# Attention probabilities of layer three transposed by DMA in two 16-bit planes instead of by TensorE

## The reference

```
def _cross_attention(q_in, kv_in, wq, bq, wk, bk, wv, bv, wo, bo, bias_k, bias_v):
    b, q_len, _ = q_in.shape
    t = kv_in.shape[1]
    qh = (q_in @ wq + bq).reshape(b, q_len, H, K)
    kh = (kv_in @ wk + bk).reshape(b, t, H, K)
    vh = (kv_in @ wv + bv).reshape(b, t, H, K)
    kh = jnp.concatenate([kh, jnp.broadcast_to(bias_k, (b, 1, H, K))], axis=1)
    vh = jnp.concatenate([vh, jnp.broadcast_to(bias_v, (b, 1, H, K))], axis=1)
    logits = jnp.einsum('bqhk,bthk->bhqt', qh, kh) / scale
    weights = jax.nn.softmax(logits, axis=-1)
    ctx = jnp.einsum('bhqt,bthk->bqhk', weights, vh).reshape(b, q_len, H * K)
    return ctx @ wo + bo
```

## Time and profile before

| | |
|---|---|
| median of 3 runs | 2156.26 us (2155.0 to 2164.39) |
| profiled execution, its own time | 2160.24 us |
| its span | 2158.5 us |
| mean granted clock of TensorE | 0.965 of full speed |
| PE / PEld / DVE / ACT / POOL busy | 90% / 76% / 50% / 44% / 33% |
| items of layer three's attention | 128, scores from 500 to 1554 us |

### The profile page before, as it was taken

How to read it: one execution, slowest core, us unless ns; L and a number is a source line. 1 busy time by engine, 2 the same in 40 slices (tenths; PEclk the granted TensorE clock), 3 DMA queues, 4 the chain that set the end, 5 groups by cost and what they waited for, 6 DMA issues and landing times.

```text
span 2158.5 us, 39293 instructions
## 1 busy us (share of the span) xinstructions
PE 1932.7 (90%) x16097; PEld 1644.8 (76%) x16097; DVE 1080.9 (50%) x1979; ACT 956.9 (44%) x2550; POOL 707.7 (33%) x819
## 2 busy tenths in 40 slices
PE   6788887898999999999999999999989788878798
PEld 4566665786888888888888888888867666657587
DVE  4444544544444444455554444445443577686743
ACT  4244333333444444343434443444434467666633
POOL 3322222402232413234233241323321367666500
PEclk9899998999999999999999999999999899999899
DMA  3000001100000000000001010000020000000000
GB/s 107 10 7 2 7 2 41 57 1 20 10 30 1 30 11 11 21 1 21 11 19 42 1 40 1 17 14 1 20 87 1 10 2 1 7 1 6 1 19 22
DMA packets 28035, 38.45 MB, mean 18 GB/s; under 512 B 1344, under 2 KB 19408, under 8 KB 27856
## 3 DMA queue, kind: packets, MB, share of 16 engines
q1 hardware_dynamic: 27856, 35.95, 5.2%
HBM read 33.84 MB, written 2.10 MB: 17 GB/s over the span
## 4 chain that ended last, share of the span: by engine, by line
PE 77%; DVE 10%; ACT 8%; issue 3%; POOL 1%; DMA 0%; ACTq 0%; SPq 0%; DVEq 0%; POOLq 0%
PE ps_high L196 40%; PE ps_four L196 7%; PE ps_four L2613 5%; PE ps_four L2633 5%; PE ps_four L2622 2%; PE ps_four L2417 2%; PE ps_high L2509 2%; PE ps_high L2400 1%; ACT l_pt L1717 1%; PE ps_four L2425 1%; PE ps_four L2539 1%; PE ps_high L2438 1%; ACT l_pt L1759 1%; DVE l_sm L2134 1%; PE ps_four L2549 1%
## 5 line engine op out<-in xcount | busy, mean ns | idle before, releaser
L1813 ACT ACTIVATE l_prob<-ps_four,l_mx 128x129 f32<-128x129 f32 x512 | 181.7, 368 | 565.3 <-DVE l_mx L2169 565.3
L1605 POOL TENSOR_TENSOR l_prob<-l_prob,l_mx 128x516 f32<-128x516 f32 x128 | 134.4, 1050 | 723.2 <-DVE l_mx L2176 723.2
L196 PE MATMUL ps_high<-ctxT,l_wk 128*128 128x512 f32 x768 | 211.9, 412 | 0.0
L196 PE MATMUL ps_high<-l_hT,l_wq 128*128 128x512 f32 x768 | 209.8, 408 | 0.0
L196 PEld LDWEIGHTS ps_high<-l_wo,l_ao 128*128 128x128 f32 x1536 | 196.3, 189 | 14.0 <-DVE l_ao L2188 3.1
L196 PE MATMUL ps_high<-l_wo,l_ao 128*128 128x256 f32 x1536 | 202.3, 281 | 1.9 <-DVE l_ao L2188 1.9
L196 PE MATMUL ps_high<-l_wv,ctxT 128*128 128x512 f32 x768 | 201.8, 398 | 1.8 <-ACT l_qT L1794 1.4
L1571 POOL TENSOR_TENSOR l_sm<-l_sm,l_mask 128x1024 f32<-128x1024 f32 x64 | 150.3, 2370 | 119.8 <-DVE l_sm L2134 119.6
L196 PEld LDWEIGHTS ps_high<-l_wv,ctxT 128*128 128x128 f32 x768 | 143.0, 189 | 44.0 <-ACT l_qT L1794 10.3
L196 PEld LDWEIGHTS ps_high<-ctxT,l_wk 128*128 128x128 f32 x768 | 137.2, 192 | 23.1
L196 PEld LDWEIGHTS ps_high<-l_hT,l_wq 128*128 128x128 f32 x768 | 134.6, 188 | 22.9
(11 more groups left out here) (296 smaller groups left out, 3878.6 us busy)
## 6 DMA issues: line engine op xcount, KB each, us to landing
l_staging<-in_L_xattn_wv SPq DMA_DIRECT2D x8, 512.0 KB, 3.6
l_staging<-in_L_xattn_wk SPq DMA_DIRECT2D x8, 512.0 KB, 3.6
l_staging<-in_L_xattn_wq SPq DMA_DIRECT2D x8, 512.0 KB, 4.0
l_staging<-in_L_xattn_wo SPq DMA_DIRECT2D x8, 512.0 KB, 3.5
ctx_tok<-in_ctx SPq DMA_DIRECT2D x8, 256.0 KB, 3.3
x_tok<-in_x SPq DMA_DIRECT2D x4, 512.0 KB, 5.5
l_raw_w<-in_L_xattn_mlp_w SPq DMA_DIRECT2D x2, 1024.0 KB, 7.5
l_staging<-in_L_xattn_w_fc SPq DMA_DIRECT2D x4, 512.0 KB, 4.1
```

The source lines that it names most:

```text
L196: ins = e.matmul(out, a, b, start=start and i == 0, stop=stop and i == 2, skip_group_check=not check)
L1605: e.tensor_tensor(pr[:, :, 0:S + 1], pr[:, :, 0:S + 1], mx[:, 3, :].unsqueeze(2).to_broadcast([P, GB, S + 1]), ALU.mult).then_inc(sem("poo ...
L1813: ins = e.activation(pr.t[:, b, 0:S + 1], banks[b // 2].t[:, (b % 2) * (S + 2):(b % 2) * (S + 2) + S + 1], ACT.Exp, bias=mx[:, 1, b:b + 1] ...
```

## The change

The four transposes on TensorE and the copy out of PSUM go. VectorE now splits the scaled probabilities of item step-1, seen as 16-bit halves, into two planes (low and high halves), SyncE turns both by one transposing DMA of 128 x 1024 elements of 16 bits, and VectorE merges the two turned planes into `l2_probT` in the next step. To make room, the buffers for queries and keys become one each instead of two; there is one buffer for the planes and one for the turned planes.

The order in a step is new. After the scores (step-1) come the low part of the output of item step-3 (`rest`), the merge (step-2), the query and the key projection (step), the normalisation and the split into planes (step-1), the output projection of item step-3, one batch of V, and the values (step-2) last. Since GpSimd writes the key columns with the stage of the key projection, these now stand ahead of its scaling. The weight loads are issued by ScalarE instead of SyncE, and the next weights are asked for two items earlier. The layer normalisations' transposes use bank 2 alone. In the second attention one bias matmul of 256 columns stands in place of two of 128. `x_bias` now waits for the bias loads of each layer.

```diff
-        QT = self.ring("l2_qT", 2, [P, T], F32, scope)
-        KT = self.ring("l2_kT", 2, [P, GB, S + 2], F32, scope)
+        QT = self.ring("l2_qT", 1, [P, T], F32, scope)
+        KT = self.ring("l2_kT", 1, [P, GB, S + 2], F32, scope)
+        planes = [Slot(sb("l2_planes" + n, [P, 2, GB, S], U16)) for n in ("", "T")]
...
-            if g == 1 and h == 0 and nxt[0] < 2 and nxt not in wslots:
+            if g == 0 and h == 2 and nxt[0] < 2 and nxt not in wslots:
...
+        self.tr = self.banks(2)
...
         for step in range(N + 2):
             if 1 <= step <= N:
                 scores(step - 1)
+            if 3 <= step:
+                rest(step - 3)
+            if 2 <= step:
+                merge(step - 2)
             if step < N:
                 project(step, "q")
+            if step < N:
+                project(step, "k")
+            else:
+                next(mlp)
+                next(mlp)
             if 1 <= step <= N:
                 normalise_rows(step - 1)
-            if 2 <= step <= N + 1:
-                values(step - 2)
+                transposes(step - 1)
+            if 3 <= step:
+                output(step - 3)
+            advance(weights_ahead, 1)
+            advance(norms_ahead, 4 if step < 12 else 2)
+            project(step - 2, "v")
             if step >= N:
                 next(mlp)
                 next(mlp)
-            advance(weights_ahead, 1)
-            advance(norms_ahead, 4 if step < 12 else 2)
-            if step < N:
-                project(step, "k")
-            project(step - 2, "v")
-            if 2 <= step <= N + 1:
-                output(step - 2)
-            if step >= N:
-                next(mlp)
-                next(mlp)
-            if 1 <= step <= N:
-                transposes(step - 1)
+            if 2 <= step:
+                values(step - 2)
+        rest(N - 1)
+        output(N - 1)
         self.barrier("l3")
...
+        def l2_tr(n):
+            f = pl.info["l2_tr", n]
+            q.wait_ge(*pl.done("dve.l2_planes", n))
+            q.wait_ge(*(pl.done("dve.l2_merge", n - 1) if n else pl.event(f["free"])))
+            e.dma_start(self.planes[1][:].rearrange("p i b t -> p (i b) t"), self.planes[0][:].rearrange("p i b t -> p (i b t)"),
+                        transpose=True).then_inc(sem("sp.l2_tr"), 16)
...
+        def l2_planes(n):
+
+            q.wait_ge(*pl.done("pool.l2_norm:n", n))
+            q.wait_ge(*(pl.event(pl.info["l2_tr", n - 1]["landed"]) if n else pl.event(pl.info["l2_planes", n]["free"])))
+            e.tensor_copy(self.planes[0][:], use["l2_prob", n].t[:, :, 0:S].bitcast(U16).rearrange(
+                "p b (t i) -> p i b t", i=2)).then_inc(sem("dve.l2_planes"), 1)
+
+        def l2_merge(n):
+            pt = use["l2_probT", n]
+            q.wait_ge(*pl.event(pl.info["l2_tr", n]["landed"]))
             q.wait_ge(*pl.event(pt.before))
-            e.tensor_copy(pt.t[:], bk.t).then_inc(bk.slot.empty, 1)
+            e.tensor_copy(pt.t[:].bitcast(U16).rearrange("p (b t i) -> p b t i", b=GB, i=2),
+                          self.planes[1][:].rearrange("p i b t -> p b t i")).then_inc(sem("dve.l2_merge"), 1)
...
-        def l2_tr(n):
-            pr = use["l2_prob", n].t
-            q.wait_ge(*pl.done("pool.l2_norm:n", n))
-            bk = fill("l2_tr", n)
-            for b in range(GB):
-                ins = e.transpose(bk.t[:, b * S:(b + 1) * S], pr[:, b, 0:S], self.ident[:])
-            ins.then_inc(bk.slot.full, 1)
```

More of the change, by code:

```diff
@@ L784, in plan_l2_attention @@
         hT = [Ring([Slot(sb("l2_hT3", [P, 2, DC, T], F32R))])]
-        QT = self.ring("l2_qT", 2, [P, T], F32, scope)
-        KT = self.ring("l2_kT", 2, [P, GB, S + 2], F32, scope)
+        QT = self.ring("l2_qT", 1, [P, T], F32, scope)
+        KT = self.ring("l2_kT", 1, [P, GB, S + 2], F32, scope)
+        planes = [Slot(sb("l2_planes" + n, [P, 2, GB, S], U16)) for n in ("", "T")]
+        self.planes = [s.t for s in planes]
         PR = self.ring("l2_prob", 2, [P, GB, S + 2], F32, scope)
         late = [s for k in (PT, AO, pbT, hT[0], QT, KT, PR) for s in k.slots]
+        late += planes
         hT2 = Ring([Slot(sb("l2_hT2", [P, 2, DC, T], F32R))])
@@ L839, in load_mlp_weights @@
                 i = staging.slots.index(pl.use["l2_staging", "l2m", name, part].slot)
-                pl.emit("m_w_load", name, part, landed=self.dma(f"sp.l2_staging{i}"))
+                pl.emit("m_w_load", name, part, landed=self.dma(f"act.l2_staging{i}"))
                 for half in range(2):
@@ L921, in transposes, with merge @@
         def transposes(n):
-            pl.bank(tr_ring, "l2_tr", n)
+            pl.emit("l2_planes", n, free=planes[0].freed if n == 0 else None)
+            pl.free("l2_prob", n, by=("dve.l2_planes", n))
+            pl.emit("l2_tr", n, landed=self.dma("sp.l2_tr"), free=planes[1].freed if n == 0 else None)
+        def merge(n):
             pl.slot(PT, "l2_probT", n)
-            pl.emit("l2_tr", n)
-            pl.free("l2_tr", n)
-            pl.free("l2_prob", n, by=("full", "l2_tr", n))
+            pl.emit("l2_merge", n)
         def values(n):
@@ L938, in values, with rest @@
                 pl.free("V", n - h, by=("full", "l2_values", n))
+        def rest(n):
+            pl.emit("l2_rest", n)
+            pl.free("l2_values", n)
         def output(n):
@@ L1371, in l2_loads @@
             e.dma_start(self.l2m_b2[:], a["L2_xattn_b_fc2"].partition_broadcast(P)).then_inc(sem("sp.l2m_bias"), 16)
[L1373 to L1387, removed]
-                src = a["L2_xattn_w_fc1"].rearrange("(c p) n -> p c n", p=P)[:, :, part * F // 2:(part + 1) * F // 2]
-            else:
-                src = a["L2_xattn_w_fc2"].rearrange("(c p) n -> p c n", p=P)[:, part * FC // 2:(part + 1) * FC // 2, :]
-            e.dma_start(u.t[:].rearrange("p (c n) -> p c n", c=src.shape[1]), src).then_inc(
-                sem(pl.info["m_w_load", name, part]["landed"][1]), 16)
+        def l2_tr(n):
[4 more added lines that the diff above has]
+                        transpose=True).then_inc(sem("sp.l2_tr"), 16)
         def l3_loads():
@@ L1824, in l2_values, with l2_w_load, m_w_load @@
                 sem("act.l2_values"), 1)
+        def l2_w_load(k, at, hg):
+            u, n = use["l2_staging", k, at, hg], str(at + 1)
+            q.wait_ge(*pl.event(u.before))
+            if k == "wo":
+                src = self.a["L2_xattn_wo" + n][hg * HG * K2:(hg + 1) * HG * K2, :].rearrange("(c p) n -> p c n", p=P)
+                dst = u.t[:].rearrange("p (c n) -> p c n", c=HG)
+            else:
+                src = self.a[f"L2_xattn_{k}{n}"].rearrange("(c p) n -> p c n", p=P)[:, :, hg * HG * K2:(hg + 1) * HG * K2]
+                dst = u.t[:].rearrange("p (c n) -> p c n", c=DC)
+            e.dma_start(dst, src).then_inc(sem(pl.info["l2_w_load", k, at, hg]["landed"][1]), 16)
+        def m_w_load(name, part):
+            u = use["l2_staging", "l2m", name, part]
+            q.wait_ge(*pl.event(u.before))
+            if name == "w1":
+                src = self.a["L2_xattn_w_fc1"].rearrange("(c p) n -> p c n", p=P)[:, :, part * F // 2:(part + 1) * F // 2]
+            else:
+                src = self.a["L2_xattn_w_fc2"].rearrange("(c p) n -> p c n", p=P)[:, part * FC // 2:(part + 1) * FC // 2, :]
+            e.dma_start(u.t[:].rearrange("p (c n) -> p c n", c=src.shape[1]), src).then_inc(
+                sem(pl.info["m_w_load", name, part]["landed"][1]), 16)
         def l2_pbT(at, g):
@@ L2627, in l2_values @@
             v, pt = use["V", n - h].t, use["l2_probT", n].t
-            q.wait_ge(*pl.event(("empty", "l2_tr", n)))
+            q.wait_ge(*pl.done("dve.l2_merge", n))
             for b in range(GB):
@@ L2671, in l2_out_bias @@
             n = self.items.index((at, H2 // HG - 1, g, 0))
-            pt, parts = use["pbT", at, g].t, 2 if at else 1
+            pt = use["pbT", at, g].t
             q.wait_ge(*pl.event(("empty", "l2_pbT", at, g)))
@@ L2676, in l2_out_bias @@
                 bk = use["side", ("l2", n), b // 2]
-                for c in range(parts):
-                    lo = c * D // parts
-                    ins = e.matmul(bk.t[:, (b % 2) * D + lo:(b % 2) * D + lo + D // parts], pt[:, b, :],
-                                   self.BWs[:, lo:lo + D // parts], start=False, stop=True, skip_group_check=True)
+                ins = e.matmul(bk.t[:, (b % 2) * D:(b % 2 + 1) * D], pt[:, b, :], self.BWs[:], start=False, stop=True,
+                               skip_group_check=True)
             ins.then_inc(sem("pe.l2_out_bias"), 1)
```

27 lines of the change are left out of this document (12 added, 15 removed).

## The result

The changed kernel takes 2088.21 us in the median of four runs (2083.72 to 2094.77), the kernel before 2159.62 us on the same chips (2155.0 to 2164.39): the ratio is 0.9672, 95% interval 0.9635 to 0.9708. The profiled execution has a span of 2082.0 us.

A forecast was written before the change was run, and what follows sets the result against it. TensorE's own work was taken to bound the attention steps. The terms -55 - 8 + 0 + 3 + 3 + 3 gave -54 us, so 2106 us against the profiled execution and 2102 us against the median; range 2085 to 2255 us.

The forecast's parts named there:

- Transposes, -55 us: Layer three's attention: four transposes per item leave TensorE, 0.43 us in each of 128 steps, all on the path.
- VectorE copies: Split into planes and merge on VectorE: 0.69 us each, at most 1.38 us; no bound by VectorE's sum.
- The transfer: Transposing DMA between split and merge: taken as 3.3 us from issue, like a 256 KB load; bounds 2.0 and 7.5 us.
- The loop: Merge, reciprocal, scaling, split and transfer come round once a step: 2.9 us + L, 6.3 us, under TensorE's 7.37 us.
- The first rival: The loop becomes the bound from L = 4.9 us, making the kernel slower, about 2260 to 2450 us; chance 0.26.
- L: Time from the split's end to the turned data being there, SP's issue included; taken as 3.4 us.
- Small stalls, -8 us: Steps after an x addition: V's 0.40 us wait for the query evacuation shrinks, some 30 x 0.25 us back.
- normalisations, 0: Normalisation steps: the wait for the values' bank goes, waits for ScalarE's copy come; set against each other, within 10 us.
- Key columns first: GpSimd writes the key columns ahead of its scaling: costs nothing, moves 0.2 us ahead of a wait.
- GpSimd +3: VectorE's split meets GpSimd's weight splits and both slow: loop 7.0 to 7.6 us in half the steps, +3 us.
- loads +3: Weight loads on ScalarE's queue: issue hidden, but sharing DMA engines they can hold up a transfer, +3 us.
- Tail, +3 us: After the last scores, little covers the two copies, the transfer and the output's added step: about 3 us longer.

The follow-up runs named there:

- a_pe_transposes: Changed kernel with planes, transfer and merge taken out and TensorE's four transposes put back behind the values: stage 1028.4 us, ratio to before 0.9869.
- p_out_of_order: Changed kernel with a plain transfer, the split writing both planes in turn in the order of its reads: stage 1074.5 us, ratio to before 1.0102.
- a_no_transfer: Changed kernel without the transposing transfer, the merge reading the unturned planes, both VectorE copies kept: stage 983.8 us, ratio to before 0.9669.
- p_weights_on_sp: Changed kernel with a plain transfer, weight loads issued by SyncE again instead of ScalarE: stage 981.9 us, ratio to before 0.9624.

## Why the prediction was right or wrong

The sign and the mechanism (TensorE bounds the stage, the transfer stays hidden) were right, the size a quarter too small. In part the nearness is luck, as errors of opposite sign cancel: the transposes gave 10 us less than the sum has, the order 17 us more than its 8, and the terms for GpSimd, loads and tail were 9 us of loss where the stage shows 2 at most and the tail a gain of 3. By its steps:

- **Transposes, -55 us.** Right in a plain step: 7.81 became 7.40 us in the traced one, and in the new order the eleven plain sums are shorter by 0.44 us a step without the transposes. Over the stage, moving the transposes is worth 44.6 us in the new order, as the normalisation steps keep only 6 of their 17 us: PE stands still 5.9 us longer than in a_pe_transposes and the granted clock falls again. That VectorE's extra copies delay these steps is likely, not shown. In the old order it is 36.5 us. "All of it lies on the path" was the part that failed.
- **VectorE copies.** Right: 0.694 and 0.684 us against 0.69. By the rule of the Trainium skill ("VectorE: DVE Perf Modes", What auto-detection actually checks) the mode with both ports holds for both copies, and the trace agrees with the lower bound. But the copy of p_out_of_order meets the same conditions (one source, both sides in SBUF, an outermost size of 4 on both) and took 2.87 us, so here the measurement decides. What sets it apart is that its 16-bit elements are written to two planes in turn, which the prediction did not consider.
- **The transfer.** Right: 3.1 us from issue against 3.3. The prediction's estimate of 10.5 us was eight times the 1309 ns that the Trainium skill ("VectorE: DVE Perf Modes", The three transpose paths) gives for one block. The trace does not bear it out for eight blocks in one transfer: they cost 0.8 us more than a plain transfer.
- **The loop.** Right in form, shown by two and three transfers; its fixed part is 2.6, not 2.9 us, and the threshold against the old step 5.2 us instead of 4.9. The first rival never came near: L was 3.2, and it would have needed 5.2.
- **Small stalls, -8 us, and normalisations, 0 "within 10 us either way".** This is the term that was mis-sized most. The order with the transposes kept is worth 25.4 us: 2.8 in the plain sums, where the small stalls lie, and 22.6 in the sums with normalisations, which the prediction had at nothing. Of the waits for the values' bank only one, of 2.02 us, was read; there were six, 14.1 us in all. The bank alone brought 9.2 us. That the waits also go with a lower granted clock (0.94 against 1.00 in the first 30 us of the stage) was in none of the terms.
- **Key columns first, "costs nothing".** It costs nothing, and that misses the point: without it the other parts lose 35.5 us. The prediction priced the step moved, not what the step's old place would have cost in the new kernel.
- **GpSimd +3, loads +3.** Without any transfer the stage is as long (a_no_transfer), so a longer loop and held-up transfers cost it nothing. With the loads on SyncE it is 2.0 us shorter (p_weights_on_sp). The prediction read from the earlier trace rows that such a pair slows both engines. In that trace only VectorE's operation is long (1.46 us, 0.41 in the median of its 24); GpSimd's 1.28 is its usual time. In the changed kernel it is the other way: the split took 693 to 696 ns in all 128 items, and GpSimd's small copy beside it is the one that got longer.
- **Tail, +3 us.** It was 3 us the other way: from the last scores to the next layer's first load 25.2 us before, 22.2 us after (1484.1 to 1506.3). The order does it: in a_pe_transposes, without any transfer, it is 22.7 us already (1528.7 to 1551.4).

## What to carry to other kernels

Work taken from the bounding engine is only worth its own time if the waits behind it move too: here the old order would have returned a third of it (36.5 of 55 us), and the order with all transposes kept was worth 25 us. A transfer between two engines' steps was free here as long as the loop through it (2.6 us + L) was shorter than the step. Find that loop in the engines' program order: it left less room for L (4.7 us) than the one-way path did (7.7 us). When a step of the program shrinks, price every unmoved neighbour again: a 0.2 us copy left behind a weight split cost 35 us.

## What was not expected of the hardware

- A VectorE copy of 128 x 1024 16-bit elements takes 0.69 us when it reads every second element and writes in order, 0.68 us when it reads from two places in turn and writes in order, and 2.87 us when it reads in order and writes to two planes in turn. Each is one access pattern, so which feature of the last one costs the time is not shown.
- GpSimd's copy of 128 x 4 elements, started 0.03 us after a VectorE copy from SBUF to SBUF, lasts as long as that copy: 0.71 us beside 0.69 and 2.88 beside 2.87 (medians), where it takes 0.19 in the kernel before, which has no such copy there. The rows of all 128 in the changed kernel and in p_out_of_order:
```profile
L1610 POOL COPY l_pb<-l_prob x128: 710/712/716, 506.3 to 1492.2; 128x4 f32<-128x4 f32 x128
```
```profile
L1609 POOL COPY l_pb<-l_prob x128: 2748/2877/3245, 508.5 to 1585.3; 128x4 f32<-128x4 f32 x128
```
- One transposing transfer of eight 128 x 128 blocks costs SyncE 1.23 us of issue and lands after 3.0 to 5.3 us (median 3.1); a plain one within SBUF costs 0.46 us and lands after 2.3 us.
